# Halo copies of the int8-level convolution: issued from ScalarE's queue instead of SyncE's

## Time and profile before

| | us |
|---|---|
| median of 3 runs | 3791.02 (3787.89 to 3796.55) |
| the profiled execution's own time | 3767.42 |
| its span | 3765.6 |
| busy: PE, DVE, ACT, POOL | 2979.5, 3117.7, 1893.1, 1490.4 |

### The profile page before, as it was taken

One profiled execution on the slowest core, in us unless ns is written; L12 is line 12 of the kernel. 1 busy time (PEld: TensorE's weight loads), 2 busy tenths in 40 slices (PEclk: granted clock), 3 DMA queues, 4 the chain that ended last, 5 costly groups with the idle time before them and its releaser, 6 DMA issues.

```text
span 3765.6 us, 126495 instructions
## 1 busy us (share of the span) xinstructions
PE 2979.5 (79%) x45732; PEld 2646.9 (70%) x45732; DVE 3117.7 (83%) x5880; ACT 1893.1 (50%) x2799; POOL 1490.4 (40%) x1984
## 2 busy tenths in 40 slices
PE   0000004899999999999999989999999999999998
PEld 0000002788888888888888878888888888888888
DVE  8999994688878888888888878888888888888876
ACT  8999981344444444444444434444444444444443
POOL 4777000344334344343343334333433433333444
PEclk9999999999999999999999999999999999999999
DMA  8767650366666666666666656666666666666655
GB/s 309 241 236 242 236 188 16 118 196 198 198 188 196 197 195 197 194 192 195 199 194 191 195 178 194 194 192 195 192 194 191 196 192 194 193 199 191 198 179 179
DMA packets 630696, 730.98 MB, mean 194 GB/s; under 512 B 76752, under 2 KB 602160, under 8 KB 614736
## 3 DMA queue, kind: packets, MB, share of 16 engines
q1 hardware_dynamic: 482640, 588.71, 48.6%
q10 hardware_dynamic: 147456, 134.28, 12.7%
HBM read 262.58 MB, written 134.22 MB: 105 GB/s over the span
## 4 chain that ended last, share of the span: by engine, by line
PE 50%; SPq 16%; issue 11%; DMA 11%; DVE 9%; ACT 1%; POOL 1%; ACTq 1%; DVEq 0%; POOLq 0%
PE y_ps L985 12%; PE mean_b L1030 10%; SPq L454 9%; PE conv_ps L1017 7%; PE x_ps L972 6%; DMA stack<-xn 5%; PE fin_ps L1004 5%; SPq L376 4%; PE t_ps L963 3%; DMA out<-img 3%; PE conv_ps L1019 3%; DVE scaled L758 2%; DMA img<-in_x 2%; PE fin_ps L999 2%; DVE scaled L759 1%
## 5 line engine op out<-in xcount | busy, mean ns | idle before, releaser
L729 POOL TENSOR_SCALAR eo<-img,norm 128x256 f32<-128x256 f32 x512 | 481.5, 940 | 1502.1 <-PE t_ps L963 1274.2
L985 PEld LDWEIGHTS y_ps<-mix_w,stack 128*128 128x128 f16 x24576 | 787.5, 99 | 158.1 <-DMA stack<-xn 84.6
L985 PE MATMUL y_ps<-mix_w,stack 128*128 128x64 f16 x24576 | 810.4, 194 | 62.4 <-DMA stack<-xn 62.0
L540 ACT ACTIVATE xt<-t_ps 128x512 f32<-128x512 f32 x512 | 305.8, 597 | 910.8 <-PE t_ps L963 802.9
L554 ACT ACTIVATE y_hi<-y_ps 128x512 f16<-128x512 f32 x512 | 305.8, 597 | 535.4 <-PE y_ps L985 534.4
L834 DVE SCALAR_TENSOR_TENSOR img<-conv_ps,cst,img 128x512 f32<-128x512 f32 x512 | 382.3, 747 | 226.9 <-PE conv_ps L1019 226.4
L821 DVE SCALAR_TENSOR_TENSOR xn<-x_ps,norm,xn 128x512 f16<-128x512 f32 x512 | 383.1, 748 | 220.7 <-ACT xn L547 215.6
L1030 PE MATMUL mean_b<-row_mean,img 128*128 128x48 f32 x4096 | 538.2, 275 | 16.6 <-DVE img L834 16.2
L972 PE MATMUL x_ps<-dft,xt 128*128 128x128 f32 x4096 | 543.0, 276 | 0.0
L1030 PEld LDWEIGHTS mean_b<-row_mean,img 128*128 128x128 f32 x4096 | 511.3, 196 | 31.7 <-DVE img L834 31.5
L972 PEld LDWEIGHTS x_ps<-dft,xt 128*128 128x128 f32 x4096 | 499.7, 192 | 0.1
(11 more groups left out here) (134 smaller groups left out, 5138.9 us busy)
## 6 DMA issues: line engine op xcount, KB each, us to landing
stack<-xn SPq DMA_DIRECT2D x2048, 132.0 KB, 2.6
img<-in_x SPq DMA_DIRECT2D x1024, 128.0 KB, 2.8
out<-img ACTq DMA_DIRECT2D x1024, 128.0 KB, 3.0
img<-in_x SPq DMA_DIRECT2D x120, 1024.0 KB, 4.9
halo<-quant SPq DMA_DIRECT2D x192, 193.3 KB, 3.3
halo<-quant SPq DMA_DIRECT2D x64, 169.1 KB, 3.0
row_mean<-table_row_mean SPq DMA_DIRECT2D x1, 768.0 KB, 15.4
spread<-table_spread SPq DMA_DIRECT2D x1, 512.0 KB, 14.4
```

The lines of the kernel that those rows point to most:

```text
L729: nc.gpsimd.tensor_scalar(even, rows[:, :, 0:F], norm[v][:, 2:3], None, ALU.add).then_inc(shift_s, 1)
L985: last = nc.tensor.matmul(y_ps[t % 2][:, g, b, :], stack[:, t % 2, g, first:first + F], mix_w[:, 2 * at + b, g, f, part, :], start=i == 0, ...
```

## The change

`halo_rows` moves from SP's program to ACT's, with the same waits, copies and semaphores, now on ACT. In a step it comes after `y_high(t+1)` and ahead of the small image steps and of `store(t-2)`. The two chunks of sample 0 that were issued by SP ahead of the loop are issued by ACT after its ten `scale_pair` calls.

```diff
--- before.py
+++ after.py
@@ -428,20 +428,6 @@
                     sp.sem_inc(tick_s, 1)
                     load(u, u, q)
 
-            def halo_rows(k, c):
-
-                sp.wait_ge(quant_s, PAIRS * k + QP * (c + 1))
-                sp.sem_inc(tick_s, 1)
-                sp.wait_ge(conv_s, PAIRS * k + QP * min(c + 2, QU))
-                sp.sem_inc(tick_s, 1)
-                lo, hi = QB * c, QB * c + QB
-                for side, rows, f, l, to in ((0, slice(R - 1, P, R), lo, min(hi, HB - 1), lo + 1),
-                                             (1, slice(0, P - R + 1, R), max(lo, 1), hi, max(lo, 1) - 1)):
-                    run = (l - f) * HW - 2
-                    src = quant_f[rows, f * HW:f * HW + run]
-                    src = bass.AP(src.tensor, src.offset, [list(src.ap[0]), [1, 3], [1, run]])
-                    sp.dma_start(halo_f[48 * side:48 * side + 48, to * HW:to * HW + run], src).then_inc(halo_s[c], 16)
-
             def restack(s, t):
 
                 sp.wait_ge(mix_s, done(s, t - 2))
@@ -467,10 +453,6 @@
                         load_pair(s + 1, 1 - u, t + PAIRS - 3)
                     if runs(mix, conv, t + 3):
                         restack(s, t + 3)
-                    if t in (2, 6) and conv:
-                        halo_rows(s + 1, t // 4 + 2)
-                    if t in (10, 14) and ahead:
-                        halo_rows(s + 2, t // 4 - 2)
 
             for u in range(2):
                 for q in range(QU):
@@ -483,8 +465,6 @@
             for u in range(2):
                 for j in range(PAIRS):
                     sp.sem_inc(pair_s[u][j], 1)
-            for c in range(2):
-                halo_rows(0, c)
             periods(sp, period)
             for b in range(STORES):
                 sp.wait_ge(store_s[b], 32 * PAIRS // STORES * samples + 1)
@@ -552,6 +532,20 @@
                 act.wait_ge(mix_s, done(s, t))
                 act.wait_ge(fin_s, done(s, t - 2))
                 nc.scalar.activation(in_order(y_hi, t), y_by_group[t % 2], ACT.Copy).then_inc(yhi_s, 1)
+
+            def halo_rows(k, c):
+
+                act.wait_ge(quant_s, PAIRS * k + QP * (c + 1))
+                act.sem_inc(tick_s, 1)
+                act.wait_ge(conv_s, PAIRS * k + QP * min(c + 2, QU))
+                act.sem_inc(tick_s, 1)
+                lo, hi = QB * c, QB * c + QB
+                for side, rows, f, l, to in ((0, slice(R - 1, P, R), lo, min(hi, HB - 1), lo + 1),
+                                             (1, slice(0, P - R + 1, R), max(lo, 1), hi, max(lo, 1) - 1)):
+                    run = (l - f) * HW - 2
+                    src = quant_f[rows, f * HW:f * HW + run]
+                    src = bass.AP(src.tensor, src.offset, [list(src.ap[0]), [1, 3], [1, run]])
+                    act.dma_start(halo_f[48 * side:48 * side + 48, to * HW:to * HW + run], src).then_inc(halo_s[c], 16)
 
             def store(s, u, t):
 
@@ -577,6 +571,10 @@
                         scale_pair(i + (u + d) // 2, (u + d) % 2, jq)
                     if runs(mix, conv, t + 1):
                         y_high(s, t + 1)
+                    if t in (2, 6) and conv:
+                        halo_rows(s + 1, t // 4 + 2)
+                    if t in (10, 14) and ahead:
+                        halo_rows(s + 2, t // 4 - 2)
                     if conv and t == IMAGE_AT:
                         act.wait_ge(mean_s, s + 2)
                         nc.scalar.activation(row_t[:, 0, :], mean_ps[0], ACT.Copy)
@@ -597,6 +595,8 @@
             act.wait_ge(scale_s, 1)
             for j in range(AHEAD):
                 scale_pair(0, 0, j)
+            for c in range(2):
+                halo_rows(0, c)
             periods(act, period)
             for t in (PAIRS - 2, PAIRS - 1):
                 store(samples - 1, 1, t)
```

## The result

The changed kernel takes 3886.55 us (median of 4 runs, 3885.20 to 3892.67) against 3789.45 us of before on the same chips: a ratio of 1.0265, interval 1.0231 to 1.0300. It is 97 us slower. I had forecast 3787, with a range that ended at 3813. The profiled execution has a span of 3885.7 us, 120.1 more than that of before, which was among the fastest of its kernel (3767.42 us; its timed runs took 3773 to 3802).

What follows compares the result with a forecast made beforehand. PE was taken to set the pace, SP in part of each sample. Loop terms of -0.27 us per sample gave -8 over 30 samples, plus 4.5 at the start: -3.5, so 3764 profiled, 3787 as median; range 3765 to 3813.

Steps and rivals of the forecast that it cites:

- What bounds the kernel: Steady stretch: PE sets the pace, SP in part of each sample; a freer SP gives back at most 58.2 us.
- SP is relieved by 1.5 us in four steps, and at t = 14 the load starts 1.45 us earlier, a gain of 0.35: SP's queue: 1.5 us less in each of four steps; at t = 14, 0.35 us per sample gained, between 0 and 0.9.
- The start, +4.5: Before the loop, once: chunk 0's copies wait for the tenth scaling, so the first period moves by +4.5 us.
- Step 6, the halo waits go: At t = 6 copies begin beside the restack, so PE's waits for chunk 3 go: 0.07 us per sample gained.
- It now lands later by 1.3 us of issue: ACT's store behind the copies lands 1.3 us later; at t = 10 the load starts 0.4 later, losing 0.35 per sample.
- Rival C: Store lands 2 us later instead of 1.3, PE loses about 0.6 per sample at t = 11: about 3810 us, chance 0.23.
- I cost it at nothing, with 0.1 us per sample as the upper bound: ACT's compute behind the copies: waits for transposes cover most steps; `turn_out` up to 1.3 us late elsewhere, without cost to PE.
- Step 2, a gain of 0.15: At t = 2 SP catches up 1.5 us sooner: 0.15 us per sample gained, between 0 and 0.3.

Runs made afterwards that it cites:

- the best version: Kernel before, copies kept on SP, chunk 0's moved to step 9 and chunk 1's to step 0, loads one step later: 3719.36 us, ratio 0.9815.
- the single edits: Kernel before with only SP's copies moved (chunk 0 to step 9, chunk 1 to step 0): 3778.76 us; with only the loads one step later: 3763.98 us.

## Why the prediction was wrong, step by step

- *What bounds the kernel*: right that PE sets the pace, and SP in part of each sample. The bound of the gain, 58.2 us of stack waits, was too low: the best version is 72 us faster by medians, with 15.4 us of such waits left. (The profiles are 37 us apart; that of before is 24 us under its median and that of the best version 11 above.) What went besides the 47 us of waits I did not separate. Nor do both stalls stand behind steps 10 and 14, as I had put them: per sample PE waited 0.36 us before pair 14 and 0.57 before pair 2, but also 0.58 and 0.31 before pairs 0 and 1.
- *SP is relieved by 1.5 us in four steps, and at t = 14 the load starts 1.45 us earlier, a gain of 0.35*: SP was relieved of the issues, but the gain did not come. I had the store of step 14 land 5.3 us after `y_high` (2046.65 - 2041.35). In the mean it landed 7.17 us after it (4.50 before), and the load began 0.4 us later. It is the same late store as at step 10, mis-sized in the same way.
- *The start, +4.5*: right, 4.8.
- *Step 6, the halo waits go*: right in the loop.
- **"It now lands later by 1.3 us of issue": mis-sized.** The store's first issue began 1.77 us later (the copies took 1.40 us, and my 1.3 had no room for the 0.26 between the last copy and the store, nor for the wait and count ahead of them), its own issues became slower (1.96 for 1.60), and the bytes came on top: the load began 2.3 us later in the sample shown, 1.8 in the mean, instead of 0.4. The loss behind step 10 was 2.5 us per sample in intervals 12 and 13 instead of 0.35. Rival C had the mechanism and the point from which it decides, a store that lands 1.6 us later (in the mean it was 2.6), and I gave it 0.23. Its price for this place was too low by four times (0.6 us for 2.5), because it had neither the slower store nor the clock: PE's mix after a 2.8 us wait ran at half speed.
- **"I cost it at nothing, with 0.1 us per sample as the upper bound": wrong.** This is the step that failed outright. I took the 1.87 us that ACT waits for transposes, a mean over 422 waits, as cover in each step. At step 14 there is hardly any: `turn_out` came 1.9 us after `y_high`, just behind the store, whose issues end at 2041.56 + 1.54 = 2043.10. The 1.31 us that the row puts down to the transposes ended with ACT's program, which was issuing; it looked like cover. I named `turn_out`, `x_high`, `scale_pair`, `y_high` as what stands behind the copies, and left out `iy_hi`, which only step 15 has, and of which PE needs the result in the same step and not in the next. In the mean `turn_out` now comes 3.8 us after `y_high` instead of 1.8 at step 14, 3.7 instead of 1.7 at step 2 and 3.8 instead of 2.2 at step 10; only step 6 had cover (3.8 for 3.1). `iy_hi` comes 4.34 us after `y_high` instead of 2.29. The price was 1.8 us per sample in interval 15, 48 us of waits in all.
- *Step 2, a gain of 0.15*: wrong in sign, by the same error; 0.56 us are lost in interval 4, because `x_high` and then DVE's part of the conv are late.

Both errors have this in common: for the engine that the issues went to I answered with one figure for all steps, 1.3 us of issue and 1.87 us of cover, where the single step decided.

## What to carry to other kernels

A DMA issue on a compute engine isn't free because that engine is half idle: price it in the step where it stands, by what is due next there and who needs it within the same step, and count the waits, counts and the slower issues behind it. Ask what the moved transfer now stands in front of in its new queue, above all stores on which a load waits. Before a queue is relieved, look for the second thing it waits for, and move both: here the pair gave 72 us where the single edits gave 12 and 21.

## What the hardware showed that I had not expected

- ACT's engine stood 132.6 us in 43 waits of 3.1 us before `turn_out` behind a program that was issuing DMAs; a store's pair of issues took 1.96 us behind the copies, against 1.54 and 1.60.
- After a wait of 2.82 us the granted clock was 0.50 and a mix took 2.74 us for 1.57. With the longer waits the time at the lower clock more than doubled, from 61.5 to 135.6 us.
- Both kinds of transfer in ACT's queue take longer to land than before: copies 3.7 us in the median (3.3 from SP), stores 3.2 (3.0). So do the stack transfers of SP's queue in the four halo steps: those of pairs 1, 5, 9 and 13 take 3.4 to 3.8 us in the mean, where before it was 2.8 to 3.0; with the copies' bytes cut it was 2.6 to 3.0. The lines of the page's part 6, beside the earlier trace rows:

```profile
out<-img ACTq DMA_DIRECT2D x1024, 128.0 KB, 3.2
...
halo<-quant ACTq DMA_DIRECT2D x192, 193.3 KB, 3.7
```
